# Multiplying layer 1's fifth relation ahead of its bucket sums in a two-layer relational graph convolution

## What is computed

```
seg = dst * num_rel + etype
sums = segment_sum(x[src], seg); cnt = segment_sum(ones, seg)
mean = (sums / maximum(cnt, 1)).reshape(num_nodes, num_rel, -1)
out = einsum('nri,rio->no', mean, W) + x @ root + b
h = relu(conv(x, W1, root1, b1)); h = conv(h, W2, root2, b2)
out = layernorm(x + h)
```

## Time and profile before

| | us |
|---|---|
| median of 3 runs | 1705.36 |
| lowest, highest run | 1697.65, 1707.2 |
| span of the profiled execution | 1695.9 |
| PE, PEld busy in it | 1505.2, 1463.3 |
| DVE, ACT, POOL busy | 1032.7, 644.3, 860.0 |
| transfers of gathers (software queue), share of 16 engines | 27.9% |
| other transfers (hardware queue) | 20.8% |

### The profile page before, as it was taken

One profiled execution on the slowest core, in us unless ns is written; L12 is line 12 of the kernel. 1 busy time (PEld: TensorE's weight loads), 2 busy tenths in 40 slices (PEclk: granted clock), 3 DMA queues, 4 the chain that ended last, 5 costly groups with the idle time before them and its releaser, 6 DMA issues.

```text
span 1695.9 us, 25007 instructions
## 1 busy us (share of the span) xinstructions
PE 1505.2 (89%) x8493; PEld 1463.3 (86%) x8493; DVE 1032.7 (61%) x1525; ACT 644.3 (38%) x918; POOL 860.0 (51%) x711
## 2 busy tenths in 40 slices
PE   5995799996069999989989799799999999989996
PEld 5995799985069899989988799799999999989996
DVE  6789301241059889888988112365656565678796
ACT  3221122100046555558545002344444444456641
POOL 1111578787777777676542002454444535377550
PEclk9998899998579999999989899899999999999998
DMA  5342143300067666777554213564646556567552
GB/s 169 128 167 94 41 118 92 84 2 2 2 188 233 206 198 207 242 220 223 173 158 148 75 62 138 172 221 141 207 145 205 164 188 193 167 205 224 176 154 91
DMA packets 119931, 255.32 MB, mean 151 GB/s; under 512 B 28967, under 2 KB 91990, under 8 KB 119782
## 3 DMA queue, kind: packets, MB, share of 16 engines
q0 software_dynamic: 43840, 136.86, 27.9%
q1 hardware_dynamic: 76006, 117.35, 20.8%
HBM read 244.23 MB, written 65.87 MB: 183 GB/s over the span
## 4 chain that ended last, share of the span: by engine, by line
PE 52%; POOL 14%; DVE 13%; issue 10%; DMA 9%; ACT 2%; SPq 0%; DVEq 0%; POOLq 0%; ACTq 0%
PE prod L652 39%; POOL edge_table L468 13%; PE agg L680 11%; DVE g_low L886 3%; DMA raw<-y,index_b 3%; DMA x_rows<-in_x 3%; DMA raw<-y,index_a 3%; DVE ranks L1051 2%; DVE ranks L1046 2%; DVE edge_f L1054 2%; DVE g_high L886 1%; ACT g_high L526 1%; POOL raw L432 1%; DVE acc L893 1%; DVE one_hot L880 1%
## 5 line engine op out<-in xcount | busy, mean ns | idle before, releaser
L652 PE MATMUL prod<-w_high,h_high 128*128 128x384 f32 x2160 | 737.2, 341 | 22.0 <-DVE acc L869 12.1
L652 PE MATMUL prod<-w_low,h_high 128*128 128x384 f32 x2160 | 728.9, 337 | 0.0
L652 PE MATMUL prod<-w_high,h_low 128*128 128x384 f32 x2160 | 728.4, 337 | 0.0
L526 ACT ACTIVATE g_high<-raw 128x768 fp32r<-128x768 f32 x480 | 381.0, 840 | 301.2 <-DMA raw<-y,index_a 167.2
L652 PEld LDWEIGHTS prod<-w_high,h_high 128*128 128x128 f32 x2160 | 411.3, 190 | 25.6 <-issue 24.7
L886 DVE TENSOR_TENSOR g_low<-raw,g_high 128x768 fp32r<-128x768 f32 x320 | 294.8, 953 | 216.0 <-ACT g_high L526 166.2
L432 POOL DMA_INDIRECT raw<-y,index_a x240 | 288.1, 1200 | 248.4 <-issue 127.1
L652 PEld LDWEIGHTS prod<-w_low,h_high 128*128 128x128 f32 x2160 | 411.3, 190 | 0.0
L652 PEld LDWEIGHTS prod<-w_high,h_low 128*128 128x128 f32 x2160 | 410.0, 190 | 0.0
L432 POOL DMA_INDIRECT raw<-y,index_b x240 | 296.9, 1237 | 168.1 <-DVE g_low L886 87.5
L559 ACT ACTIVATE y_stage<-prod 128x384 f32<-128x384 f32 x280 | 137.5, 491 | 587.3 <-PE prod L652 559.2
(11 more groups left out here) (104 smaller groups left out, 503.2 us busy)
## 6 DMA issues: line engine op xcount, KB each, us to landing
y<-y_stage SPq DMA_DIRECT2D x280, 187.5 KB
w_raw<-in_w_all SPq DMA_DIRECT2D x36, 1152.0 KB
x_rows<-in_x SPq DMA_DIRECT2D x20, 375.0 KB
raw<-y,index_a POOLq DMA_INDIRECT x240
raw<-y,index_b POOLq DMA_INDIRECT x240
y<-in_x SPq DMA_DIRECT2D x1, 3750.0 KB, 14.9
y<-acc SPq DMA_DIRECT2D x10, 375.0 KB
out<-acc SPq DMA_DIRECT2D x10, 375.0 KB
```

The costliest lines, as they stand in the source:

```text
L526: act.activation(g_high[:, SLOT[i], :], raw[:, slot, :], ACT.Copy).then_inc(high_ready, 1)
L652: mm = pe.matmul(prod[:, bank, 0:HALF], left[:, k, t * P:(t + 1) * P], right[:, h, k, :], start=(k == 0 and left is h_high and right is w_ ...
```

## The change

Matrix q = 5 is taken out of the loop and runs with no bucket sums. Matrix q = 6 runs with `four_relations`: two bucket sums behind each product, so that all 40 sums of relations 1 to 4 stand in its 20 steps. DVE makes the low part of q = 5's second unit and of q = 6's first unit in whole, ahead of its wait for the table. POOL's and SP's lists stay as they were.

```
+        def four_relations(s):
+            return [("sum", k // T, k // T + 1, k % T) for k in (2 * s, 2 * s + 1)]
...
 (ACT)
-            with act.Fori(ROOT1 + 1, R - 1) as q:
-                matrix(q, q - 1, banks(0), two_relations(2 * q - 2 * ROOT1 - 2, 0))
+            matrix(ROOT1 + 1, ROOT1, banks(0))
+            matrix(ROOT1 + 2, ROOT1 + 1, banks(0), four_relations)
...
 (PE)
-            with pe.Fori(ROOT1 + 1, R - 1) as q:
-                matrix(q, banks(0), staged(q - 1), two_relations(2 * q - 2 * ROOT1 - 2, 0))
+            matrix(ROOT1 + 1, banks(0), staged(ROOT1))
+            matrix(ROOT1 + 2, banks(0), staged(ROOT1 + 1), four_relations)
...
 (DVE, ahead of dve.wait_ge(table_loaded, 32))
+            low_of_unit(unit(ROOT1 + 1, 1))
+            low_of_unit(unit(ROOT1 + 2, 0))
...
-            with dve.Fori(ROOT1 + 1, R - 1) as q:
-                matrix(q, two_relations(2 * q - 2 * ROOT1 - 2, 2 * q - 2 * ROOT1 - 1), low_at=in_parts)
+            matrix(ROOT1 + 2, four_relations, low_at=in_parts)
```

## The result

The changed kernel takes 1740.76 us (median of 4 runs, 1736.25 to 1743.93) against 1701.51 us of the kernel before (median of 4 runs, 1694.31 to 1707.2). The ratio is 1.0225, with a 95% interval of 1.0184 to 1.0267: slower, by 39 us between the medians, and the interval leaves open whether by more than 2%. Among the timed executions of all kernels here one was slow, a 4382 us execution of e12_before_turns, and its ratio leaves it out. The spans of the two profiled executions are 1736.5 and 1695.9 us, 40.6 us apart. The forecast was 1737, with 1721 to 1756 as its range.

A forecast was written before the change was run, and what follows sets the result against it. The prediction took PE as the fullest engine in the bucket stage, with DVE and POOL close behind. A later start of +47.6 us and a faster stage of -15 us gave +32 on 1705.4: 1737 us, range 1721 to 1756.

The forecast's parts named there:

- Part one: q = 5 in the scatter pause: PE runs six of twenty steps, to 423.9 us, leaving fourteen.
- Part two: Restart of q = 5 after the pause: fourteen steps remain, so the first bucket sum starts at 528.9, +47.6 us.
- Part three: Stage of 40 bucket sums with q = 6's products: POOL's work sets 197 us for 212.2, -15 us.
- Behind the stage: From q = 7 on, after the 40 bucket sums: nothing changes.
- A: Rival: all twenty steps of q = 5 fit into the pause, leaving -15 us, 1690 us; chance 0.03.
- B: Rival: landings keep the 40 bucket sums at the old 212 us, +47.6 us, 1753 us; chance 0.2.
- C: Rival: PE's clock falls in the bucket stage, +20 us on the forecast, 1757 us; sign: clock below 0.9; chance 0.1.
- D: Rival: POOL and DVE run near their floor in the bucket stage, 180 us, +15 us, 1720 us; chance 0.12.

The follow-up runs named there:

- e12_before_turns: The kernel before, with DVE's one-hot builds placed between the subtractions in every stage; ratio to the kernel before 0.9997.
- e1_early: Changed kernel with SP loading q = 5's second weight unit and issuing its stores through step 17 ahead of the scatter wait and table loads; 1695.44 us, ratio 0.9961.
- e2_weight: Changed kernel with only the load of q = 5's second weight unit moved ahead of the scatter wait, stores left behind; first bucket sum at 520.3 us.
- e8_single: Changed kernel with DVE's 120 subtractions of relations 1 to 4 replaced by one-input reductions, PE reading g_high twice; stage 197.6 us, span 1736.1 us.
- e10_turns: Changed kernel with one of DVE's one-hot builds ahead of each subtraction, instead of all three ahead of the first, throughout; stage 195.5 us, span 1734.7 us.
- e7_half: Changed kernel with the 120 gathers of relations 1 to 4 fetching 384 instead of 768 elements a row; stage 205.2 us.
- e3_mixed: e1_early with each product of q = 6 cut into six pieces of three matmuls, one ahead of each gathered tile; stage 213.5 us, ratio 0.9964.
- e5_pool: Changed kernel with one small POOL memset ahead of each of the 120 gathers of relations 1 to 4; stage 205.1 us.
- e9_pool: Changed kernel with four small POOL memsets ahead of each of the 120 gathers of relations 1 to 4; stage 206.2 us.
- e6_dve: Changed kernel with an extra 0.28 us one-input DVE reduction ahead of each of the 120 subtractions of relations 1 to 4; stage 204.0 us.

## Why the prediction was right, and where it was off

**Part one, six steps in the pause.** Right: PE stopped at the end of step 5, at 423.9 (423.9 forecast). e1_early shows that SP's list was the whole reason, and e2_weight that the stores hold PE once the weight unit does not.

**Part two, the restart.** Forecast: conversion at 476.8, step 6 at 479.4, first bucket sum at 528.9. Measured: 478.22, 480.77 and 530.2. The load took 8.4 us to the conversion where I took 7.5, just over the upper of my two bounds (8.2), and it was issued 0.5 us later. The loss at the lower clock level (5.7 us at 0.51 granted) and the fourteen steps were as priced. The term came to +48.9 us for +47.6.

**Part three, the pace of 40 buckets.** This term was mis-sized: -6.8 us for -15 us. PE was no longer the bound, as forecast, but the stage took 205.4 us where the sum of POOL's work gave 197. The mean issue of a gather was 1.33 us and not 1.30, which is some 3 us over 114 gathers. Beyond the 0.30 us ahead of each gather POOL idled some 10 us more (my estimate from its 45.5 idle us and 119 gathers), where the sum had 4 us for index copies and 2 for late landings. And the sum took one engine to be the bound where the chain shows a loop through landing, ACT, DVE and POOL. PE was busy 160.4 us where I had 132, at a granted clock of 0.89. From the same start the change of order gives only 0.5 us (e1_early). The other 6.3 us come with the late start, 2.1 of them by tiles that lay ready and the rest from no shown cause, so what this term did reach is in good part luck. The rule that the prediction cites did speak in the right direction. The Trainium skill, GPSIMD Engine Reference, section Specifications, has GpSimd's memory ports contended by VectorE instructions with two inputs; e8_single agrees, with a mean issue of 1.03 us where no such subtraction was left. I weighed it by the share of time that DVE subtracts, which made it 3 us. What counts besides is whether two subtractions stand back to back: e10_turns left their number and length alone, took the mean issue from 1.33 to 1.19 us and moved the stage by 10 us, more than the 8 us by which the term was off.

**Behind the stage** nothing changed, as forecast (1.5 us less in all).

**The total.** The change was forecast at +32 us and measured at +39 (medians) and +40.6 (spans). That the total looks closer, 1740.8 for 1737, is luck: the forecast started from 1705.4, the median of three executions of the kernel before, and with the fourth it is 1701.5.

**The rivals.** A, all twenty products in the pause, did not happen for the reason given, and e1_early shows its worth when it does: not -15 us but -5.5 (1695.4 against 1700.9 us in the same comparison), since the scatters end later and the stage runs at the old pace. B, the old pace because landings set it: the measured pace lay almost midway between the forecast and B (205.4 of 197 and 212), and e1_early came out at B's pace. B's reason is not what the runs show, since e7_half shortened the landings by 1.3 us and the stage stayed. (The row behind B has 48.9 of ACT's 60.7 us of waits as landings, four fifths and not half.) C, the clock: its sign, a clock below 0.9 in the stage, did appear (0.89), and a step took 10.3 us for the 9.8 of the forecast. e3_mixed raised the clock to 0.93 and gained nothing, but with a wait of its own, so what share of the missing 8 us the clock has is not shown. D did not happen.

**What stays open.** That POOL alone sets the 205 us is not shown: its load could not be raised by itself (e5_pool and e9_pool), and in e3_mixed and e6_dve the gathers got shorter while the stage did not, each time with another engine waiting or working more. What is shown is that the order of DVE's list moves the stage. How much of that comes by way of the shorter gathers, and how much by slots that come free earlier, is open, and so is what holds e8_single at 197.6 us. The order of e10_turns in layer 1 alone, on e1_early, might keep the 14 us of its stage without the loss in layer 2; it was not tried.

## What to carry to other kernels

Before work is moved into a pause, follow every queue that this work needs, transfers above all: here four engines' lists would have let twenty steps run, and one wait in a fifth list, ahead of a weight load and the stores, let six. Compare stages that start from the same state: tiles that lie ready at the start flatter the pace. A rearrangement that takes PE off the bound gains only down to the next engine, and that engine's price per instruction may depend on what its neighbour does at the same moment, so read the spread of its durations beside the neighbour's timeline and not only the mean. An order that helps one stage should be tried there alone: where PE is the bound, the same order only cost time (6.8 us in four matrices).

## What the runs showed of the hardware

In these traces an indirect transfer issued by POOL is held while DVE runs an instruction with two inputs in on-chip memory, and for two of them if they stand back to back: 1.00 us alone, 1.67 beside one subtraction of 0.95 us, 2.62 beside two. It holds for the scatters too. In e1_early, DVE converts a weight unit in 2.56 us during the scatter:

```profile
415.01 2.56 DVE L863 TENSOR_TENSOR w_low<-w_raw,w_high 128x2304 fp32r<-128x2304 f32 x1 [9.15 <-ACT w_high L531]
...
414.38 1.19 POOL L481 DMA_INDIRECT edge_table<-payload,position  x1 [0.30 <-issue]
415.88 2.75 POOL L481 DMA_INDIRECT edge_table<-payload,position  x1 [0.31 <-issue]
418.94 1.19 POOL L481 DMA_INDIRECT edge_table<-payload,position  x1 [0.30 <-issue]
...
444.27 1.19 POOL L481 DMA_INDIRECT edge_table<-payload,position  x1 [0.30 <-issue]
449.68 1.19 POOL L481 DMA_INDIRECT edge_table<-payload,position  x1 [4.22 <-issue]
```

The scatter begun at 415.88 took 2.75 us for 1.19. Around the second conversion, at 446.2, POOL stood 4.22 us; the kernel before has a stop of 2.35 us at the same scatter, with no conversion near:

```profile
443.59 1.18 POOL L468 DMA_INDIRECT edge_table<-payload,position  x1 [2.35 <-issue]
```

So the two conversions cost 1.6 and 1.9 us. The last scatter ended at 464.2 us in the kernel before (464.4 in the changed kernel), at 466.5 in e2_weight, with one such conversion, and at 470.3 in e1_early, with two. Not all of that is theirs: of e1_early's 6.1 us, 2.7 were already there before its first conversion, and of e2_weight's 2.3 us, 0.8, from causes that no run shows. I had not priced this in e1_early, whose conversions run during the scatter; they make 3.4 of the 5.9 us by which its first bucket sum is late.
